# Relative attention on one Trainium2 core: score blocks of 32 queries by four heads in place of 16 queries by eight

## What is computed

```
q, k, v = x @ Wq + bq, x @ Wk + bk, x @ Wv + bv          # x: layernorm of h, 256 x 128
dist    = clip(key - query, -68, 68) + 68
score   = (q . k + q . rel_k[dist]) / sqrt(128)           # per head
out     = softmax(score) @ v + sum_key softmax * rel_v[dist]
h       = h + out @ Wo + bo
```

## Time and profile before

| what | value |
|---|---|
| median of 3 runs (lowest, highest) | 1922.81 us (1922.19, 1923.03) |
| the profiled execution: span from first to last instruction, its own time | 1922.3 us |
| PE busy over the span | 1656.3 us, 86% |
| DVE, ACT, POOL busy over the span | 1402.0 us, 938.9 us, 882.1 us |
| granted TensorE clock, mean | 0.942 |
| content matmuls (L1707) | 1536, three groups of 512 |
| SP's reads of `q_rep` | 256 of 64.0 KB |

### The profile page before, as it was taken

One profiled execution on the slowest core, in us unless ns is written; L12 is line 12 of the kernel. 1 busy time (PEld: TensorE's weight loads), 2 busy tenths in 40 slices (PEclk: granted clock), 3 DMA queues, 4 the chain that ended last, 5 costly groups with the idle time before them and its releaser, 6 DMA issues. The chain is left out here.

```text
span 1922.3 us, 59270 instructions
## 1 busy us (share of the span) xinstructions
PE 1656.3 (86%) x21927; PEld 1392.3 (72%) x21927; DVE 1402.0 (73%) x3369; ACT 938.9 (49%) x2305; POOL 882.1 (46%) x1710
## 2 busy tenths in 40 slices
PE   5999999999979884999599999999999999648750
PEld 4888888888858773999478888888888888525430
DVE  6777777877758884666787888888888888635434
ACT  2222212221228770677467777777777777424320
POOL 3333333333202566566232455445555555547771
PEclk9999999999989995999699999999999999869985
DMA  8900000000022001222323333333333333256537
GB/s 298 165 0 0 0 0 0 0 0 0 0 81 102 23 25 55 65 72 65 124 60 63 74 87 78 77 77 78 76 79 80 86 77 78 63 149 171 169 102 271
DMA packets 312667, 147.60 MB, mean 77 GB/s; under 512 B 205238, under 2 KB 291284, under 8 KB 312020
## 3 DMA queue, kind: packets, MB, share of 16 engines
q1 hardware_dynamic: 299876, 118.38, 25.3%
q0 software_dynamic: 12544, 25.91, 3.9%
HBM read 72.03 MB, written 73.37 MB: 76 GB/s over the span
## 5 line engine op out<-in xcount | busy, mean ns | idle before, releaser
L2143 POOL DMA_INDIRECT x_slots<-rel_x,rel_at x128 | 135.5, 1059 | 212.5 <-PE rel_s_ps L1727 186.9
L535 PE MATMUL tok_main_ps<-tok_w_h,tok_feat_h 128*128 128x512 f32 x512 | 205.3, 401 | 0.9 <-DVE tok_feat_low L99 0.9
L1966 ACT ACTIVATE rel_e<-rel_s_ps,rel_neg_max 128x255 f32<-128x255 f32 x512 | 200.2, 482 | 10.7 <-DVE rel_neg_max L2299 9.5
L535 PE MATMUL tok_main_ps<-tok_w_h,tok_feat_l 128*128 128x512 f32 x512 | 200.6, 392 | 0.0
L535 PE MATMUL tok_main_ps<-tok_w_l,tok_feat_h 128*128 128x512 f32 x512 | 200.3, 391 | 0.0
L2299 DVE TENSOR_REDUCE rel_neg_max<-rel_s_ps 128x4 f32<-128x1020 f32 x128 | 155.9, 1218 | 53.2 <-PE rel_s_ps L1727 51.2
L84 POOL TENSOR_TENSOR tok_q_pre<-tok_v_q,tok_v 128x128 f32 (+1 forms) x32 | 39.0, 1219 | 310.5 <-DVE tok_q L274 295.8
L1707 PE MATMUL rel_s_ps<-rel_k_h,rel_q_head_h 128*128 128x256 f32 x512 | 154.6, 302 | 0.2 <-DVE rel_q_head_l L2273 0.2
L1748 PE MATMUL rel_t_ps<-all_k_ident,rel_e 128*128 128x128 f32 x1024 | 139.3, 279 | 14.4 <-issue 14.0
L294 DVE TENSOR_TENSOR tok_prod<-tok_main_ps,tok_v 128x1024 f32<-128x1024 f32 x64 | 78.4, 1225 | 97.9 <-PE tok_main_ps L540 97.9
L1748 PEld LDWEIGHTS rel_t_ps<-all_k_ident,rel_e 128*128 128x128 f32 x1024 | 109.6, 141 | 47.0 <-issue 45.8
(11 more groups left out here) (406 smaller groups left out, 4725.2 us busy)
## 6 DMA issues: line engine op xcount, KB each, us to landing
rel_q_rep<-q_rows SPq DMA_DIRECT2D x256, 64.0 KB, 2.5
o_rows<-rel_rv SPq DMA_DIRECT2D x256, 64.0 KB
x_slots<-early_zeros SPq DMA_DIRECT2D x16, 520.0 KB, 6.2
exp_x<-x_slots SPq DMA_DIRECT2D x32, 260.0 KB, 3.0
y_rows<-early_zeros SPq DMA_DIRECT2D x16, 512.0 KB, 5.8
final_y<-y_rows SPq DMA_DIRECT2D x16, 512.0 KB, 12.0
exp_x<-x_slots SPq DMA_DIRECT2D x72, 65.0 KB, 1.9
q_rows<-rel_qT SPq DMA_DIRECT2D x64, 64.0 KB
```

The costliest lines, as they stand in the source:

```text
L535: nc.tensor.matmul(main_ps[s][:, cols], feat[fk][:, s, j, :], w_p[wk][:, j, cols], start=(j == 0 and (fk, wk) == (0, 0)), stop=False)
L1966: last = nc.scalar.activation(e[u % 2][:, n, 0:L], s_ps[u % 2][:, n, 0:L], ACT.Exp, bias=neg_max[u % 2][:, n:n + 1])
L2143: nc.gpsimd.indirect_dma_start(x1_slots[:], bass.IndirectOffsetOnAxis(ap=at[n][:, k, t:t + 1], axis=0), x1[n][:, t, k, :], None).then_inc( ...
```

## The change

A block of scores becomes 32 queries by four heads. The 128 columns of `Wq` and `Wk` are laid out twice as wide (256), each head's 16 dimensions repeated, so that a half `a` has four heads in 32 partitions each: 16 that hold the rounded query part and 16 that hold the rest. One matmul against the rounded keys and one against their rests then give all four products: 8 content matmuls of 256 columns for a unit, not 12. The keys of the two halves take the place of the two end-biased copies. Position queries are placed by the transfers themselves into a zeroed `q_pos` (128 partitions: eight positions of 16 dimensions), so that the masked product on VectorE goes, and the position matmuls use all 128 rows of the array by a strip of 32.

```
     def repeat_queries(b, r):
         sp.wait_ge(q_ready, b + 1)
-        for f in range(2):
-            sp.dma_start(q_rows[r][:, f], qT[:].rearrange("p (u f t) -> p u f t", f=2, u=NU)[:, :, f]).then_inc(q_out, 16)
-        sp.wait_ge(q_out, 32 * b + 32)
-        if after(b, 1):
-            sp.wait_ge(qp_ready, b)
-        for f in range(2):
-            for i in range(QUAD):
-                at = 64 * f + HD * i
-                sp.dma_start(q_rep[at:at + HD], q_rows[r][:, f].rearrange("(h d) u t -> d h (u t)", d=HD)).then_inc(q_in, 16)
+        if after(b, 2):
+            sp.wait_ge(s_done, NU * (b - 1))
+        sp.dma_start(q_rows[r], qT[:]).then_inc(q_out, 16)
+        sp.wait_ge(q_out, 16 * b + 16)
+        if b == 0:
+            sp.wait_ge(zeroed, 6)
+        for i in range(OCT):
+            for a in range(2):
+                sp.dma_start(q_pos[r][HD * i:HD * i + HD, a, i // QUAD, :, i % QUAD, :],
+                             q_rows[r].rearrange("(h v d) a i g -> d h v a i g", v=2, d=HD)[:, :, 0, a, i, :]).then_inc(q_in, 16)
...
     def project_k(b):                                   # project_q in the same way, with wq_sb
-        nc.tensor.matmul(pa, wk_sb[:], xT[:], start=True, stop=True).then_inc(k_done, 1)
+        for a in range(2):
+            last = nc.tensor.matmul(pa_halves[:, a, :], wk_sb[:, a * P:(a + 1) * P], xT[:], start=True, stop=True)
+        last.then_inc(k_done, 1)
...
     def content(b, u, r):
-        for n in range(UB):
-            blk = UB * u + n
-            for qk, kk in THREE:
-                nc.tensor.matmul(s_ps[u % 2][:, n, :],
-                                 q_head[r][qk][:, 4 * blk:4 * blk + 4].rearrange("p c h i -> p (c h i)"), keys_for(k_p[r][kk], u),
+        for a in range(2):
+            for q in range(2):
+                g = 4 * (2 * u + q)
+                for k in range(2):
+                    nc.tensor.matmul(s_ps[u % 2][:, 2 * a + q, :],
+                                     q_head[r][a][:, g:g + 4].rearrange("p c w h i -> p (c w h i)"), k_p[r][k][:, a, :],
...
     def position_scores(b, u, r):
         if u == 0:
-            pe.wait_ge(qp_ready, b + 1)
+            pe.wait_ge(q_in, 16 * 2 * OCT * (b + 1))
-        for k in range(2):
-            for f in range(2):
-                n = 2 * f + k
-                lo, hi = table_keys(UB * u + n)
-                for c in range(4):
-                    off = KOFF - BQ * (UB * u + n) - QUAD * c
-                    last = nc.tensor.matmul(s_ps[u % 2][32 * c:32 * c + 32, n, lo:hi],
-                        q_pos[r][64 * f:64 * f + 64, 8 * u + 4 * k + c].rearrange("p h i -> p (h i)"),
-                        table[64 * f:64 * f + 64, off + lo:off + hi], start=False, stop=True, skip_group_check=True)
+        for q in range(2):
+            for a in range(2):
+                for c in range(4):
+                    g = 4 * (2 * u + q) + c
+                    lo, hi = table_keys(u, OCT * g)
+                    off = KOFF - OCT * g
+                    last = nc.tensor.matmul(s_ps[u % 2][32 * c:32 * c + 32, 2 * a + q, lo:hi],
+                        q_pos[r][:, a, :, :, :, g].rearrange("p w h i -> p (w h i)"),
+                        table[:, off + lo:off + hi], start=False, stop=True, skip_group_check=True)
...
-def table_keys(blk):
-    if blk < NBLK // 2:
-        return 0, min(L, BQ * blk + BQ + MAX_REL - 1)
-    return max(0, BQ * blk - MAX_REL + 1), L
+def table_keys(u, q0):
+    if u < NU // 2:
+        return 0, min(L, q0 + OCT + MAX_REL - 1)
+    return max(0, q0 - MAX_REL + 1), L
...
     def read_q(b):                                      # ACT; by_octets reads PSUM with a step of 8 elements
-        for odd in range(2):
-            nc.scalar.activation(q_hl[:, 0, odd], pa, ACT.Identity, bias=q_bias[:, odd:odd + 1], scale=q_scale[:, odd:odd + 1])
-        nc.scalar.activation(qT[:], pa, ACT.Identity, bias=bq_sb[:], scale=SCALE).then_inc(q_ready, 1)
+        for a in range(2):
+            nc.scalar.activation(q_round[:, a], by_octets(pa_halves[:, a]), ACT.Identity, bias=q_bias[:, a:a + 1], scale=q_scale[:])
+        for a in range(2):
+            last = nc.scalar.activation(qT[:, a], by_octets(pa_halves[:, a]), ACT.Identity, bias=bq_sb[:, a:a + 1], scale=SCALE)
+        last.then_inc(q_ready, 1)
-    def round_queries(b, r, pairs):                     # and its calls in slots 2 and 3
-        for k in pairs:
-            nc.scalar.activation(of_heads(q_head[r][0], k), of_pair(0, k).bitcast(FP32), ACT.Copy).then_inc(qh_ready, 1)
...
-    def queries_rest(b):                                # DVE: 2 of 128x256; queries_remainder: 4 copies of 32x512
-    def position_queries(b, r):                         # and its call in slot 1
-        nc.vector.tensor_tensor(q_pos[r][:], q_rep[:].rearrange("p h (g i) -> p g h i", i=QUAD), mask4 ..., ALU.mult)
+    def split_queries(b, r, a):                         # a = 0 in slot 3 for b+2, a = 1 in slot 0 for b+1
+        for k in range(H // 2):
+            last = nc.vector.tensor_tensor(q_head[r][a][32 * k:32 * k + 32, :, :, k, :], of_head(qT, a, k),
+                                           of_head(q_round, a, k).bitcast(FP32), ALU.subtract)
+        last.then_inc(q_split, 1)
...
     def read_eT(b, u):                                  # ACT and DVE; the turned exponentials go to their blocks in runs of 16
-        nc.scalar.activation(eT[s][:, 0, n:n + UB], t_ps[:, 0], ACT.Copy).then_inc(eT_a, 1)
+        nc.scalar.activation(turned_blocks(eT[s][:, 0], u), in_blocks(t_ps[:, 0]), ACT.Copy).then_inc(eT_a, 1)
...
     # GpSimd's head: zeroes q_pos, after the stores of the first experts
+    for j in range(U0):
+        pool.wait_ge(y0_out[j], 16 * (ST0 // U0))
+    for r in range(2):
+        nc.gpsimd.memset(q_pos[r][:], 0.0).then_inc(zeroed, 1)
```

More of the change, by code:

```diff
@@ L1499, in relative_attention @@
              m.sem(n) for n in (
[L1500 to L1501 removed]
+                 "zeroed x_ready xT_done xT_ready q_done k_done q_ready kh_ready kl_ready q_split "
+                 "q_out q_in v_done v_ready s_done max_ready e_ready t_done eT_a eT_v pv_done "
                  "rv_done rv_read rv_out rv_in o_read ot_done ot_read rden_ready sum_ready o_ready oT_done oT_ready "
                  "out_done h_ready").split())
[L1504 removed]
+        odd = K["odd_sixteen"]
         gate_sb = weights.sb["gate"]
@@ new lines, in content @@
+                    for a in range(2):
[3 more added lines that the diff above has]
+                                nc.tensor.matmul(s_ps[u % 2][:, 2 * a + q, :],
+                                                 q_head[r][a][:, g:g + 4].rearrange("p c w h i -> p (c w h i)"),
+                                                 k_p[r][k][:, a, :], start=(k == 0 and q == 0), stop=False,
+                                                 skip_group_check=True)
@@ L1931, in read_k @@
                         act.wait_ge(s_done, NU * (b - 1))
-                    if b == 0:
-                        act.wait_ge(tables_made, 1)
-                    for end in range(2):
-                        last = nc.scalar.activation(k_p[r][0][:, end], pa, ACT.Identity, bias=bk_end[:, end:end + 1])
+                    act.wait_ge(set_up, 2)
+                    for a in range(2):
+                        last = nc.scalar.activation(k_p[r][0][:, a], pa_halves[:, a], ACT.Identity, bias=bk_sb[:, a:a + 1])
                     last.then_inc(kh_ready, 1)
@@ L1940, in read_q @@
                     if after(b, 1):
-                        act.wait_ge(q_out, 32 * b)
-                        act.wait_ge(rest_ready, b)
-                        act.wait_ge(qh_ready, 4 * b)
-                    else:
-                        act.wait_ge(set_up, 2)
-                    for odd in range(2):
-                        nc.scalar.activation(q_hl[:, 0, odd], pa, ACT.Identity, bias=q_bias[:, odd:odd + 1],
-                                             scale=q_scale[:, odd:odd + 1])
-                    nc.scalar.activation(qT[:], pa, ACT.Identity, bias=bq_sb[:], scale=SCALE).then_inc(q_ready, 1)
-                def round_queries(b, r, pairs):
-                    act.wait_ge(q_ready, b + 1)
-                    if after(b, 2):
-                        act.wait_ge(s_done, NU * (b - 1))
-                    act.wait_ge(set_up, 2)
-                    for k in pairs:
-                        nc.scalar.activation(of_heads(q_head[r][0], k), of_pair(0, k).bitcast(FP32), ACT.Copy)\
-                            .then_inc(qh_ready, 1)
+                        act.wait_ge(q_out, 16 * b)
+                        act.wait_ge(q_split, 2 * b)
+                    for a in range(2):
+                        nc.scalar.activation(q_round[:, a], by_octets(pa_halves[:, a]), ACT.Identity, bias=q_bias[:, a:a + 1],
+                                             scale=q_scale[:])
+                    for a in range(2):
```

(11 more changed lines are left out.)

149 lines of the change are left out of this document (57 added, 92 removed).

## The result

The changed kernel takes 2017.58 us (median of 4 runs, 2009.95 to 2021.83), the kernel before 1922.92 in the same session: ratio 1.048, 95% interval [1.0454, 1.0506]. The forecast had 1938 and a range to 1980; the time is slower, as forecast, by six times as much. The profiled execution took 2014.46 us, its span 2012.7.

A forecast was written before the change was run, and what follows sets the result against it. It took PE and ACT to set the pace in turn, SP's ring having slack: 30 batches x (0.04 + 0.42) = 13.8 us, plus 1.2 for the head, on 1922.3, gave 1938 us; 8-in-10 range 1900 to 1980.

The forecast's parts named there:

- ScalarE's part: On ACT's stretch ahead of the read PE waits for: `read_q` has four activations for three, +0.42 us a batch.
- SP's queue: One write for two and 16 reads for eight put the value rows 1.1 to 3.65 us later.
- the ring: Chain through SP, queries to value rows to `combine`: 1.0 us to spare, 0.37 gained from the product's going.
- SP's ring decides: Rival, chance 0.24: hold-ups and slow landing remain on SP's queue, +1.7 us a batch, 1975 us.
- DVE: Eight subtractions, about 0.3 us each, 2.4 us in slots 3 and 0, hidden by idle time; the masked product, 1.22, goes.
- Position scores: On PE, 128 rows by 32 for 64 by 32: 4.01 us a batch for 2.81, +1.2 us.
- Content: On PE, four matmuls fewer a unit, 0.114 us apart: -1.8 us a batch.
- PE sets the pace: From slot 3 to slot 1's position scores PE bounds the batch; the change adds +0.04 us there.
- the second projections: On PE, keys and queries each get one more 256-column projection of 0.43 us: +0.86 us a batch.
- Head: First batch's position scores wait for 16 reads, less the product's time: 0 to 2.4 us, 1.2 taken.
- Steps cost: Rival, chance 0.12: stepped PSUM reads slow `read_q` by +1.5 us, weight loads perhaps too; 1970 us.
- The faster rival: Rival, chance 0.22: freed DVE decides, scores run at 0.449 ns a column, -0.65 us a batch, 1904 us.

The follow-up runs named there:

- run 6: Changed kernel, SP's sixteen reads reordered: four while the value rows' writes land, four behind the value rows' read, nothing left out: 1980.83 us.
- run 16: Changed kernel with SP's new read order, steps turned round, and the eight subtractions spread over slots 3, 0 and 1, all work kept: 1946.19 us.
- run 12: Changed kernel with SP's new read order; VectorE takes the rests in two subtractions of 128 partitions, ScalarE places them with eight copies: 2022.75 us.
- run 9: Changed kernel with SP's new read order, three of slot 0's four subtractions left out, and position scores on 64 rows (half their sum missing): 1942.88 us.
- run 3: Changed kernel with position weights loaded from 32 neighbouring elements instead of with a step, the right order of position queries left out: 2014.39 us.
- run 8: Kernel before, with the third content matmul of each block left out, 8 matmuls in a slot for 12: 1917.36 us.
- run 11: Kernel before, with four of SP's eight reads moved to while the value rows' writes land, and eight content matmuls for 12: 1892.82 us.
- run 15: Changed kernel with SP's new read order, six of eight subtractions left out, 64-row scores, and second projections left out after the first batch: 1909.14 us.
- run 5: Changed kernel with three of slot 0's four subtractions left out, transfers as in the changed kernel: 2022.66 us.
- run 4: Kernel before, with each of SP's eight reads of repeated queries cut into two, sixteen of 32 KB: 2039.04 us.

## Why the prediction was wrong

The loss of 95 us has three layers. Two are shown by undoing them in turn with all work kept: SP's order 37 us (run 6), the place and step of the subtractions 35 (run 16). About 20 remain; PE's own sum accounts for them, but no run took them away by themselves. That the time moved the way that was forecast is luck in the main: of the forecast's 15 us ScalarE's part came true, and most of the loss stands where the sum had nothing.

- **SP's queue: the step that failed first.** The text had the value rows 1.1 to 3.65 us later, the ring's period changed "by -0.2 to +2.3 us", and took "the lower part, since the reads get smaller". The delay is 3.63 us, the upper end. The 0.92 us by which the eight reads had been held up was booked as relief from smaller reads; sixteen small ones are held up as well, 8.46 to 9.66 us where sixteen times 0.456 are 7.3. The faster way of the value rows behind them did come (from their first write to their read 3.42 and 3.76 us, for 4.55), and the reads ate it. The slack was too large as well: it took the landing of the queries' reads, 2.5 us, for that of the value rows, which is 2.86 (1212.07 to 1214.93), and so 0.6 was to spare. With that and the 0.37 for the product's going, 3.63 gives +2.7 a batch where the period grew by 2.93; undoing the order alone brought 1.1 back, since the next layer then showed. The rival "SP's ring decides" was the right one, at 0.24; it was priced at +1.7 a batch, since it counted the reliefs and the gain from the product's going.
- **DVE: "about 0.3 each, 2.4 us, in slots 3 and 0; DVE idles for 18 of 100 us, and that hides them".** Wrong twice. Each took 0.68, eight 5.4 us, for 2.7 us that the work they replaced had taken (L2261 and L2273 of the kernel before, twice 0.486 and four times 0.438). The 0.3 came from a row of 1024 elements scaled down to 256; 418 ns is what 256 take without a step (run 12), and the kernel before has a subtraction of that size (L99, `tok_inc_l`) at 413 ns. From 418 to 681 ns the runs do not take apart: reads with a step of 128 bytes, writes in runs of 16 bytes and 32 partitions came together. And idle time in the sum hides nothing: both groups stood ahead of the maxima, on the chain from scores to exponentials. Their place counted for more than their cost (run 16).
- **Position scores: mis-sized**, 4.01 taken, 4.16 as the upper bound, 4.41 measured. The neighbours in the shape of 128 rows, 0.449 and 0.483 ns a column, were quicker than the scores became, 0.512; the 64 rows bring the old pace back (run 9), the step in the weights is not why (run 3), and what makes the scores slower than their neighbours is open. The Trainium skill, "TensorEngine Tiling (Array Packing)", Overview, gives up to 2 times where a dimension is at most 64; the measured ratio is 1.57.
- **Content: right in size, wrong in what it buys.** Still 32 matmuls a batch at 0.114 us; but in the kernel before it buys 6 us alone and 27 with the ring eased (runs 8, 11). "PE sets the pace" was right only as far as the ring's slack.
- **ScalarE: right.** `read_q` takes 1.64 us by starts (1219.41 to 1221.05) for 1.26; +0.38 where +0.42 was forecast. Its PSUM read with a step of eight elements costs nothing.
- **Head: mis-sized.** The first projection of the steady stage comes 3.2 us later; the text took 1.2, from a range of 0 to 2.4.
- **The rivals.** "Steps cost" named the wrong places: neither `read_q` nor the weight loads, but the subtractions, which read with a step of 128 bytes. The rule of the Trainium skill ("SBUF — State Buffer", The DMA port swizzle) that each access that crosses to a new line of 16 bytes pays a penalty fits 418 against 681 ns; how much of the difference is the step no run shows. The faster rival fell, since the freed VectorE was filled again and the scores' new shape was slower than its neighbours, not as quick.

Not tried: how much of the remaining 20 us the second projections hold by themselves, which run 15 left open.

## What to carry to other kernels

Count a queue's issues, not its bytes, and ask what stands behind them: eight more small transfers ahead of a short round trip cost 37 us here, more than the 27 that the matmuls saved were worth at best (run 11), and interleaving them with the waits of that trip took the 37 back. Size an instruction from a row with the same column count and the same steps, and look at what stands right behind it on its engine; idle time summed over a stretch hides nothing that lies ahead of a chain. Undo causes together as well as singly: run 5 alone would have acquitted the subtractions, and run 8 the content. And read the granted clock of each run first: in runs 4, 5 and 8 the waits brought a lower clock with them, and the time holds both.

## What was unexpected of the hardware

- Reads of 8 KB, 32 KB and 64 KB go out of SP's queue at about the same pace: sixteen of 8 KB in 8.46 to 9.66 us, sixteen of 32 KB in 8.04 to 9.55 (run 4), eight of 64 KB in 4.57.
- A 256-column fp32 subtraction takes 418 ns on 128 partitions without a step, and 681 on 32 partitions with reads 128 bytes apart and writes in 16-byte runs; ScalarE's copy into the same places needs as long (2.71 us for four). The Trainium skill, "VectorE: DVE Perf Modes", The TRN2 errata, gives (N + 151) / 0.96 ns for an fp32 add of two tensors; for 256 columns that is, as an estimate, 424 ns, and the unstepped row agrees.
- A weight load with a step of 128 bytes takes 165 ns in place of 113, and the matmuls' pace doesn't show it.
- In run 4 PE worked at half its clock from 1214 to 1219 us, right behind a wait of 3.85 us: 64 matmuls took 1.94 us in place of 1.10. So a wait can cost PE more than its own length.
